# A language-model tower: values product with swapped operands on 32-column tiles, second bias in the accumulation, second norm on ScalarE

## The chip, the cores and the metric

The program runs on one core of one Trainium2 chip. The metric is the device time of one execution in microseconds; three timed executions of the kernel before gave 2760.56, 2769.51 and 2775.77 us, median 2769.51. The engines are named PE (TensorE, matrix products into PSUM), DVE (VectorE), ACT (ScalarE), POOL (GpSimd) and SP (SyncE, which starts DMAs).

## The reference

32 sequences of 512 tokens, each with 128 features, go through an embedding, three attention and feed-forward layers, and a routed expert layer:

```python
h = encoded(byte embedding, hashed 3- to 8-gram embeddings)      # 6 gathers of 128 floats per token
X = layernorm(h)
for l in range(3):
    Xn = layernorm(X) * ln1_w + ln1_b
    Q, K = rotary(Xn @ WQ), rotary(Xn @ WK); V = Xn @ WV         # 4 heads of 32 features
    A = (Q @ K.T) * decay mask                                   # causal, no softmax
    Y = A @ V                                                    # per head
    Yn = (Y - mean) / sqrt(var + eps), per head, * gn_w + gn_b
    G = Xn @ WG
    Y = (G * sigmoid(G) * Yn) @ WO + X
    X = gelu(layernorm2(Y) @ w1 + b1) @ w2 + b2 + Y
h = h + X
out = h + expert[argmax(layernorm(h) @ Wg + bg)](layernorm(h))   # 8 experts, 128 -> 256 -> 128
```

All of it is fp32. Means are taken out of the weights ahead of time (the output projection, w2, b2 and V's weights are centred), so a norm in the layers needs only a mean of squares.

## The kernel before

**Tiling.** A sequence is four chunks of 128 tokens, and two sequences are in flight: stream s = 0, 1 takes the sequences 2*it + s for it = 0..15 ("pairs"). Each stream is worked in two halves h of two chunks each. So there are four interleaved work lines (s, h), and 16 x 3 x 4 = 192 passes of one half through one layer. Each half has two PSUM banks, a and b. The state of earlier chunks (K transposed times V, 128x128, masked to the heads) carries attention from chunk to chunk; within a chunk the scores are computed and masked.

**One layer of one half** is `attend` and then `feed`, written once per engine:
- DVE normalises X (L860), PE transposes it, ACT copies it with weight and bias to `xT` (L674).
- PE: Q and K, V, and the gate (L1154 to L1158). DVE: rotary products (L920 to L924) and the swish `sw` (L928). ACT: V and the tanh (L682, L683).
- PE transposes Q and K (L1165); ACT copies them out, Q four times with one head's rows kept (L686, L688). PE computes the state (V and K), then the scores (128x512 per chunk); DVE masks both (L934 to L945).
- PE, values (from L1178): per chunk, the product with the state, and then for each head the masked scores `A` (128x128, the stationary operand) with V's 32 columns moving, accumulated in bank a. Tokens lie on partitions.
- ACT squares y (L693), DVE sums the squares per head (L950), POOL adds eps and takes the power -1/2 (L606, L607), DVE multiplies y with it into `xn` (L954), PE transposes it, ACT applies gn_w and gn_b into `zp` (L697), DVE multiplies with `sw` (L960), PE multiplies with WO, DVE adds X into `Y1` (L963).
- `feed`: ACT square sums of Y1 (L667), POOL power (L579), DVE norm (L860), PE transposes, ACT copy; PE w1 into both banks, ACT gelu (L712), PE w2 into bank a; POOL adds the second bias to Y1 into `Y1b` (L616); DVE adds bank a and Y1b into X (L975).

**Order.** Every engine runs its stages in a fixed order, found when the program is built: `by_progress` (L380) always takes the stage with the smallest point next. A stage is what stands between two `yield`s; the yielded number is its point within `attend` or `feed`, to which the start of the part and the lag of the half (`START`, `HLAG`, L59 and L60) are added; `attend` is 29.8 and `feed` 14.4 long (L369). Beside the layers run `embed` (gathered rows summed, transposed, encoded, normed) and `route` (router norm, logits, places, scatter), and on POOL the gathers (L561), 12 per half and pair. Engines meet only at semaphores (`wait_ge`, `then_inc`); an engine that waits holds all that is behind it in its order.

**Around the layers.** Until the first gathered rows arrive the engines hash the n-grams and prepare weights (DVE L754 to L857). After the last pair, 40 tiles of 512 rows go through the experts in loops.

All PE matmuls of this text have L1097 in the profile (the helper `mm`), the transposes L1116 or L1165, so they are told apart by their tiles, written out<-moving,stationary.

## Time and profile before

| | |
|---|---|
| median of the timed runs | 2769.51 us |
| the profiled execution: its own time | 2767.15 us |
| span, first to last instruction | 2765.3 us |
| granted TensorE clock, mean | 0.972 |
| PE busy | 2505.9 us (91%) |
| PEld (weight loads) busy | 2123.8 us (77%) |
| DVE busy | 2042.8 us (74%) |
| POOL busy | 1984.1 us (72%) |
| ACT busy | 1557.8 us (56%) |

The span is what one profiled execution took between its first and last instruction. Busy is the time covered by an engine's instructions; a matmul's record runs from its start to its modelled end, so records of successive matmuls overlap. PEld runs beside PE. A line in a group of instructions gives their number behind an x and the mean duration of one in ns.

### The profile page before, as it was taken

The page shows a single profiled execution, that of the slowest core. Times are in us where ns is not written, and L with a number is a line of the kernel's source. Part 1 is how long each engine was busy: PE and PEld are TensorE (multiplying, and loading weights), DVE is VectorE, ACT ScalarE, POOL GpSimd, SP SyncE. Part 2 cuts the span into 40 slices and gives each one's busy share as a digit, 9 for nine tenths or more (in the row PEclk, how much of TensorE's full clock was granted, in tenths as well). Part 3 has the DMA queues.
Part 4 walks back from the last instruction along what each step waited for, and adds up shares of the span by engine and source line. Part 5 has one row for each costly group of instructions (what it writes and reads, how often), then busy time and mean ns, then how long its engine had stood idle before and what let it go on. Part 6 is the DMA issues. An engine that isn't in the chain of part 4 may idle for free.

```text
span 2765.3 us, 49055 instructions
## 1 busy us (share of the span) xinstructions
PE 2505.9 (91%) x16336; PEld 2123.8 (77%) x16336; DVE 2042.8 (74%) x6261; ACT 1557.8 (56%) x4733; POOL 1984.1 (72%) x2286
## 2 busy tenths in 40 slices
PE   0499999999999999999999999999999999977775
PEld 0378888888888888888888888888888888865553
DVE  5368888888787878787878887887888797764443
ACT  0156666666666666666666666666666666542332
POOL 4787777777777787868787777777787854445666
PEclk9799999999999999999999999999999999988897
DMA  4521110202021202111111112020211000003443
GB/s 158 203 72 58 61 63 27 95 25 98 26 95 29 95 27 73 49 61 63 60 62 61 62 41 81 25 98 27 95 29 33 27 17 22 7 8 108 141 133 105
DMA packets 107320, 181.25 MB, mean 66 GB/s; under 512 B 23748, under 2 KB 46406, under 8 KB 106960
## 3 DMA queue, kind: packets, MB, share of 16 engines
q1 hardware_dynamic: 73296, 110.87, 11.8%
q0 software_dynamic: 33792, 67.45, 8.3%
q8 instruction: 125, 2.05, 0.3%
q14 instruction: 107, 0.88, 0.1%
HBM read 89.54 MB, written 90.78 MB: 65 GB/s over the span
## 4 chain that ended last, share of the span: by engine, by line
PE 68%; POOL 14%; DVE 7%; issue 6%; another core or an unknown queue 2%; DMA 1%; ACT 1%; SPq 1%; POOLq 0%; ACTq 0%; DVEq 0%
PE psum L1097 61%; POOL grams L568 6%; PE psum L1116 4%; POOL gr L607 3%; PE psum L1165 3%; POOL side_rstd L586 1%; POOL routed_rows L627 1%; POOL rstd L579 1%; DVE hid L945 1%; DMA grams<-expert_w 1%; DVE side_n L874 1%; ACT sq L693 1%; PE psum L1111 1%; DVE xn L860 0%
## 5 line engine op out<-in xcount | busy, mean ns | idle before, releaser
L568 POOL DMA_INDIRECT grams<-gram_table,idx_all x768 | 780.0, 1016 | 195.5 <-issue 184.5
L1097 PE MATMUL psum<-xT,lw 128*128 128x256 f32 x1920 | 487.9, 385 | 11.9 <-ACT xT L674 8.5
L1097 PE MATMUL psum<-lw,hid 128*128 128x129 f32 x3072 | 409.6, 276 | 1.7 <-ACT hid L712 1.7
L579 POOL TENSOR_TENSOR rstd<-ss,con 128x2 f32<-128x2 f32 x320 | 230.3, 720 | 251.4 <-ACT squares L667 230.8
L1097 PE MATMUL psum<-qm,qkT 128*128 128x512 f32 x768 | 371.8, 607 | 23.6 <-DVE kv L934 21.0
L1097 PEld LDWEIGHTS psum<-lw,hid 128*128 128x128 f32 x3072 | 381.6, 192 | 9.0 <-ACT hid L712 3.8
L1097 PE MATMUL psum<-V,hid 128*128 128x32 f32 x3072 | 383.0, 269 | 5.7 <-issue 3.2
L1097 PEld LDWEIGHTS psum<-V,hid 128*128 128x128 f32 x3072 | 375.1, 192 | 12.8 <-issue 12.1
L1097 PEld LDWEIGHTS psum<-xT,lw 128*128 128x128 f32 x1920 | 339.7, 193 | 50.2 <-ACT xT L674 13.0
L712 ACT ACTIVATE hid<-psum,par 128x256 f32<-128x256 f32 x768 | 317.9, 474 | 49.8 <-PE psum L1097 44.3
L607 POOL TENSOR_TENSOR gr<-ms,con 128x8 f32<-128x8 f32 x192 | 324.6, 1691 | 16.0
L688 ACT ACTIVATE qm<-psum,con 128x256 f32<-128x256 f32 x768 | 303.5, 497 | 0.0
L1097 PE MATMUL psum<-lw,xT 128*128 128x256 f32 (+1 forms) x1536 | 293.5, 335 | 0.7 <-ACT xT L674 0.7
L674 ACT ACTIVATE xT<-psum,par 128x256 f32<-128x256 f32 x384 | 213.0, 564 | 132.7 <-PE psum L1116 129.5
L945 DVE TENSOR_TENSOR hid<-psum,con 128x512 f32<-128x512 f32 x384 | 258.4, 687 | 27.8 <-PE psum L1097 20.3
L1097 PEld LDWEIGHTS psum<-lw,xT 128*128 128x128 f32 x1536 | 257.8, 196 | 25.8 <-ACT xT L674 1.1
L1116 PE MATMUL psum<-con,xn 128*128 128x128 f32 x1152 | 223.9, 281 | 21.8 <-DVE xn L860 14.9
L693 ACT ACTIVATE sq<-psum 128x256 f32<-128x256 f32 x192 | 73.8, 384 | 279.3 <-PE psum L1097 254.6
L1097 PEld LDWEIGHTS psum<-qm,qkT 128*128 128x128 f32 x768 | 131.8, 192 | 122.4 <-issue 119.4
L1116 PEld LDWEIGHTS psum<-con,xn 128*128 128x128 f32 x1152 | 154.3, 153 | 76.3 <-DVE xn L860 32.3
L897 DVE SCALAR_TENSOR_TENSOR side_n<-grams,gate,side_n 128x128 f32<-128x128 f32 x640 | 193.3, 359 | 0.0
L667 ACT ACTIVATE squares<-Y 128x129 f32<-128x129 f32 x384 | 117.6, 315 | 119.0 <-DVE Y L963 101.0
(176 smaller groups left out, 4832.7 us busy)
## 6 DMA issues: line engine op xcount, KB each, us to landing
routed_rows<-pad SPq DMA_DIRECT2D x265, 264.0 KB
grams<-expert_w SPq DMA_DIRECT2D x44, 321.0 KB
grams<-gram_table,idx_all POOLq DMA_INDIRECT x768
grams<-routed_rows SPq DMA_DIRECT2D x44, 264.0 KB
xb<-x SPq DMA_DIRECT2D x32, 256.0 KB
lw<-layer_w SPq DMA_DIRECT2D x1, 2503.5 KB, 12.0
routed_rows<-row,slot POOLq DMA_INDIRECT x128
con<-consts SPq DMA_DIRECT2D x1, 1339.5 KB, 6.0
```

The lines of the kernel that those rows point to most:

```text
L568: pool.indirect_dma_start(grams[s][:, g, c, :], None, gram_table, bass.IndirectOffsetOnAxis(ap=idx_all[:, g, at:at + 1], axis=0))\
L579: pool.tensor_tensor(rstd[s][:, CS[h]], ss[s][:, CS[h]], const("half")[:, 0:2], ALU.pow)\
L607: pool.tensor_tensor(gr[s][:, c], ms[s][:, c], const("half")[:, 0:n], ALU.pow).then_inc(y_r[s], 1)
L667: last = act.activation(scratch[s][:, c, :], src[s][:, c, 1:], ACT.Square, scale=float(H) ** -0.5, accum_out=dst[s][:, c:c + 1])
L674: act.activation(xT[s][:, TS[h]], src[:, 0:2 * P], ACT.Identity, bias=b, scale=w).then_inc(xT_s[s][h], 1)
L688: last = act.activation(qm[s][:, h, n, :], bank_b(s, h)[:, 0:2 * P], ACT.Copy, scale=const("heads")[:, n * HD:n * HD + 1])
L693: act.activation(sq[s][:, CS[h], :], chunks(bank_a(s, h))[:, 0:2, :], ACT.Square, scale=float(HD) ** -0.5).then_inc(y_sq[s], 1)
L712: last = act.activation(hid[s][:, h, 2 * m + f, :], src[:, f * 2 * P:(f + 1) * 2 * P], ACT.Gelu, bias=param("ffn_b1", l * FB + 2 * m + f))
L897: last = dve.scalar_tensor_tensor(acc[:, c, :], grams[s][:, g, c, :], w, acc[:, c, :], ALU.mult, ALU.add)
L945: dve.tensor_tensor(A[s][:, h, m], chunks((a, b)[m]), causal.unsqueeze(1).to_broadcast([P, HEADS, P]), ALU.mult).then_inc(sc_s[s], 1)
L1097: return pe.matmul(dst, lhsT, rhs, start=start, stop=stop)
L1116: last = pe.transpose(dst[:, (c % 2) * P:(c % 2 + 1) * P], src[:, c, :], eye)
```

## The change

- **Values product.** The operands are swapped: V's 32 columns of a head are stationary, the head's 128x128 masked scores move, and the result is written to that head's 32 partitions of bank a. y now lies transposed (features on partitions, tokens along the row). The state product is swapped likewise and moved ahead of both chunks.
- **Norm of y.** The sum of squares per head is a matmul of `sq` with four columns of the head mask; DVE adds eps; POOL takes the power; ACT spreads the result over each head's 32 columns into `xn`; PE transposes that; ACT multiplies it with gn_w; DVE multiplies it with y (bank a) and then adds gn_b and multiplies with `sw`.
- **Second bias.** In setup DVE splits the centred bias into three bf16 parts, one per partition 0 to 2 of `bias2`. After the w2 matmuls, two bf16 matmuls with a stationary matrix whose first three rows are ones add it in the accumulation. POOL's add is gone and DVE adds Y1 itself.
- **Second norm** (`feed`): applied by ACT in two instructions of 128 columns instead of by DVE in one of 256.
- **Stage points.** One number per layer instead of one for all in `attend` and `feed`; other points in `embed`, `route` and the later gathers; lags written out per half. The lengths of the parts are unchanged.

```diff
-START = (0, 28.01)
-HLAG = 12.18
+LATER_GATHERS = (8.16, 13.29, 18.32, 29.07, 53.32, 54.86, 60.54, 79.31, 82.83, 96.37, 105.71, 109.59)
+LAGS = ((0, 12.38), (28.17, 40.59))
...
# gpsimd: gathered
-                    yield (1.25 * n - 15, 4.2 * n, 9.5 * n)[min(it, 2)]
+                    yield (1.25 * n - 15, 4.2 * n, LATER_GATHERS[n])[min(it, 2)]
# gpsimd: attend
-                yield -2.74
+                yield (2.93, -3.28, -3.65)[l]
...
                 pool.wait_ge(y_ms[s], nth(k, 2, h))
-                link(pool.tensor_scalar(ms[s][:, c], ms[s][:, c], EPS, 1.0, ALU.add, ALU.mult))
                 pool.tensor_tensor(gr[s][:, c], ms[s][:, c], const("half")[:, 0:n], ALU.pow).then_inc(y_r[s], 1)
# gpsimd: feed
-                yield 4.41
-                pool.wait_ge(y1_s[s], nth(k, 2, h))
-                pool.tensor_tensor(Y1b[s][:, CS[h], :], Y1[s][:, CS[h], 0:WIDE],
-                                   param("ffn_b2", l, WIDE).unsqueeze(1).to_broadcast([P, 2, WIDE]), ALU.add)\
-                    .then_inc(y1b_s[s], 1)
# scalar: new helper, and attend
+            def norm_apply(s, h, src, scale):
+                for c in half_chunks(h):
+                    last = act.activation(xn[s][:, c, :], src[s][:, c, 1:WIDE], ACT.Copy, scale=scale[s][:, c:c + 1])
+                last.then_inc(n_out[s][h], 1)
...
-                yield 21.47
-                act.wait_ge(yT_p[s], nth(k, 2, h))
-                act.activation(zp[s][:, TS[h]], bank_b(s, h)[:, 0:2 * P], ACT.Identity,
-                               bias=param("gn_b", l), scale=param("gn_w", l)).then_inc(z_a[s], 1)
+                yield (24.89, 24.28, 23.58)[l]
+                act.wait_ge(y_r[s], nth(k, 2, h))
+                act.activation(xn[s][:, CS[h], :].rearrange("p c (n d) -> p (c n) d", d=HD),
+                               gr[s][:, h * n:(h + 1) * n].unsqueeze(2).to_broadcast([P, n, HD]), ACT.Copy)\
+                   .then_inc(y_rb[s], 1)
+                yield (27.81, 27.37, 25.91)[l]
+                act.wait_ge(rT_y[s], nth(k, 2, h))
+                act.activation(zp[s][:, TS[h]], bank_b(s, h)[:, 0:2 * P], ACT.Copy,
+                               scale=param("gn_w", l)).then_inc(z_a[s], 1)
# scalar: feed
-                yield 1.18
+                yield (-71.44, 3.64, 4.99)[l]
+                act.wait_ge(n_rstd[s][h], nth(it, OWN, 2 * l))
+                norm_apply(s, h, Y1, rstd)
+                yield (5.94, 5.85, 8.36)[l]
                 norm_T(it, s, 2 * l + 1, h, bank_b(s, h), param("ln2_w", l), param("ln2_b", l))
# vector: setup
+                rest = param("ffn_b2")
+                for n in range(3):
+                    link(dve.tensor_copy(bias2_part[n][:, :], rest))
+                    if n < 2:
+                        link(dve.tensor_tensor(bias2_rest[:, :], rest, bias2_part[n][:, :], ALU.subtract))
+                        rest = bias2_rest[:, :]
+                link(dve.tensor_scalar(bias2[:, :], bias2_part[0][:, :], eye[:, 0:1], None, ALU.mult))
+                for n in (1, 2):
+                    link(dve.scalar_tensor_tensor(bias2[:, :], bias2_part[n][:, :], eye[:, n:n + 1], bias2[:, :],
+                                                  ALU.mult, ALU.add))
+                link(dve.tensor_scalar(below_three[:, :], const("vocab"), 3.0, None, ALU.is_lt))
+                dve.tensor_scalar(three_bf[:, :], ones_bf[:, :], below_three[:, :], None, ALU.mult)
# vector: attend
-                dve.wait_ge(y_sq[s], nth(k, 2, h))
-                dve.tensor_reduce(ms[s][:, h * n:(h + 1) * n], sq[s][:, cs, :].rearrange("p c (n d) -> p (c n) d", d=HD),
-                                  axis=AX_X, op=ALU.add).then_inc(y_ms[s], 1)
-                yield 18.66
-                dve.wait_ge(y_r[s], nth(k, 2, h))
-                dve.tensor_tensor(xn[s][:, cs, :].rearrange("p c (n d) -> p (c n) d", d=HD),
-                                  a[:, 0:2 * P].rearrange("p (n d) -> p n d", d=HD),
-                                  gr[s][:, h * n:(h + 1) * n].unsqueeze(2).to_broadcast([P, n, HD]), ALU.mult)\
-                   .then_inc(y_n[s], 1)
+                dve.wait_ge(ms_p[s], nth(k, 2, h))
+                dve.tensor_scalar(ms[s][:, h * n:(h + 1) * n], a[:, 2 * P:2 * P + n], EPS, None, ALU.add)\
+                   .then_inc(y_ms[s], 1)
...
-                dve.tensor_tensor(zp[s][:, ts], zp[s][:, ts], sw[s][:, ts], ALU.mult).then_inc(z_s[s], 1)
+                link(dve.tensor_tensor(zp[s][:, ts], a[:, 0:2 * P], zp[s][:, ts], ALU.mult))
+                dve.scalar_tensor_tensor(zp[s][:, ts], zp[s][:, ts], param("gn_b", l), sw[s][:, ts], ALU.add, ALU.mult)\
+                   .then_inc(z_s[s], 1)
# vector: feed
-                dve.wait_ge(n_rstd[s][h], nth(it, OWN, 2 * l))
-                norm_apply(s, h, Y1, rstd)
...
-                dve.tensor_tensor(X[s][:, cs, 0:WIDE], wide(bank_a(s, h)), Y1b[s][:, cs, :], ALU.add).then_inc(x_s[s], 1)
+                dve.tensor_tensor(X[s][:, cs, 0:WIDE], wide(bank_a(s, h)), Y1[s][:, cs, 0:WIDE], ALU.add).then_inc(x_s[s], 1)
# tensor: attend
                 pe.wait_ge(kv_s[s], nth(k, 2, h))
+                pe.wait_ge(sc_s[s], nth(k, 4, 2 * h))
+                for c in half_chunks(h):
+                    if c:
+                        mm(a[:, chunk(c % 2)], kv[s][:, c - 1, :], qkT[s][:, h, 0, c % 2, :], c < 3, False)
                 for c in half_chunks(h):
                     i = c % 2
                     pe.wait_ge(sc_s[s], nth(k, 4, c))
-                    if c:
-                        mm(a[:, chunk(i)], qkT[s][:, h, 0, i, :], kv[s][:, c - 1, :], True, False)
                     for n in range(HEADS):
-                        last = mm(a[:, i * P + n * HD:i * P + (n + 1) * HD], A[s][:, h, i, n, :],
-                                  V[s][:, c, n * HD:(n + 1) * HD], c == 0, c == 0 or n == HEADS - 1)
+                        d = slice(n * HD, (n + 1) * HD)
+                        last = mm(a[d, chunk(i)], V[s][:, c, d], A[s][:, h, i, n, :], False, i == 1)
                 last.then_inc(y_p[s], 1)
-                yield 20.53
-                pe.wait_ge(y_n[s], nth(k, 2, h))
+                yield (22.81, 20.21, 20.43)[l]
+                pe.wait_ge(y_sq[s], nth(k, 2, h))
+                for c in half_chunks(h):
+                    last = mm(a[:, 2 * P + c % 2 * HEADS:2 * P + (c % 2 + 1) * HEADS], sq[s][:, c, :],
+                              const("heads").rearrange("p (n d) -> p n d", d=HD)[:, :, 0])
+                last.then_inc(ms_p[s], 1)
+                yield (26.25, 26.56, 25.13)[l]
+                pe.wait_ge(y_rb[s], nth(k, 2, h))
...
-                half_transposes(b, xn[s], h).then_inc(yT_p[s], 1)
+                half_transposes(b, xn[s], h).then_inc(rT_y[s], 1)
# tensor: feed
+                for i in range(2):
+                    last = mm(wide(a)[:, i, :], three_bf[:, :], bias2[:, l * WIDE:(l + 1) * WIDE], False, i == 1)
                 last.then_inc(ff_p[s], 1)
```

## Rows read from the trace of the kernel before

**Rows 1.** Busy time of each engine by stretch (x instructions), granted clock, DMA share
```profile
core 0: us, PE busy (x) PEld busy (x) DVE busy (x) ACT busy (x) POOL busy (x), PEclk, DMA share, GB/s
0.00:82.00 82.00, 5.55 (x20) 3.79 (x20) 43.83 (x143) 2.96 (x8) 41.01 (x46) 1.00 0.52 193
200.00:2240.00 2040.00, 1991.59 (x13359) 1712.37 (x13357) 1643.94 (x5014) 1284.15 (x4011) 1568.47 (x1836) 1.00 0.17 56
2465.00:2765.00 300.00, 203.27 (x1045) 148.58 (x1044) 127.07 (x443) 82.25 (x138) 178.08 (x174) 0.85 0.39 114
```
**Rows 2.** The page: the chain that ended last, by engine
```profile
PE 68%; POOL 14%; DVE 7%; issue 6%; another core or an unknown queue 2%; DMA 1%; ACT 1%; SPq 1%; POOLq 0%; ACTq 0%; DVEq 0%
```
**Rows 3.** The page: the values product's group (busy, mean ns, idle before)
```profile
L1097 PE MATMUL psum<-V,hid 128*128 128x32 f32 x3072 | 383.0, 269 | 5.7 <-issue 3.2
```
**Rows 4.** PE in order of time, 1241 to 1244 us: start, length, group
```profile
1241.93 0.17 PE L1097 MATMUL psum<-pick_bf,before_bf 128*128 128x16 bf16 x1
1241.96 0.17 PE L1097 MATMUL psum<-pick_bf,ones_bf 128*128 128x16 bf16 x1
1241.98 0.47 PE L1097 MATMUL psum<-kv,qkT 128*128 128x128 f32 x2
1242.29 0.98 PE L1097 MATMUL psum<-V,hid 128*128 128x32 f32 x8
1243.10 0.47 PE L1097 MATMUL psum<-kv,qkT 128*128 128x128 f32 x2
1243.40 0.98 PE L1097 MATMUL psum<-V,hid 128*128 128x32 f32 x8
1244.22 1.96 PE L1097 MATMUL psum<-qm,qkT 128*128 128x512 f32 x4
```
**Rows 5.** PE in order of time, 1224 us
```profile
1224.06 0.51 PE L1097 MATMUL psum<-par,side_T 128*128 128x8 f32 x4
1224.43 0.81 PE L1097 MATMUL psum<-lw,hid 128*128 128x129 f32 x5
```
**Rows 6.** PE in order of time, 37 to 39 us
```profile
37.04 1.51 PE L1103 MATMUL psum<-con,hid 128*128 128x128 f32 x6 [37.04 <-DVE hid L814]
38.48 0.69 PE L1097 MATMUL psum<-par 128*64 128x128 f32 x2
```
**Rows 7.** Waits, 200 to 2240 us: who for whom, total us, times, longest
```profile
PEld psum L1116 <- DVE xn L860: 21.6, 37, 1.5
PEld psum L1097 <- DVE zp L960: 9.8, 36, 1.3
PEld psum L1097 <- ACT xT L674: 9.1, 13, 0.7
```
**Rows 8.** DVE groups, 200 to 2240 us
```profile
L960 DVE TENSOR_TENSOR zp<-zp,sw 128x256 f32<-128x256 f32 x167 | 70.7, 423 | 9.9 <-ACT zp L697 9.9
L954 DVE TENSOR_TENSOR xn<-psum,gr 128x256 f32<-128x256 f32 x167 | 69.7, 418 | 79.2 <-POOL gr L607 77.8
L950 DVE TENSOR_REDUCE ms<-sq 128x8 f32<-128x256 f32 x167 | 69.6, 417 | 82.5 <-ACT sq L693 80.2 <-issue 0.2
L860 DVE TENSOR_TENSOR xn<-Y,rstd 128x256 f32<-128x256 f32 x167 | 69.2, 414 | 0.8 <-POOL rstd L579 0.8
```
**Rows 9.** ACT groups, 200 to 2240 us
```profile
L667 ACT ACTIVATE squares<-Y 128x129 f32<-128x129 f32 x336 | 102.7, 314 | 103.4 <-DVE Y L963 85.9 <-issue 13.8
L682 ACT ACTIVATE V<-psum 128x256 f32<-128x256 f32 x167 | 64.2, 384 | 159.2 <-PE psum L1097 155.1 <-issue 4.1
```
**Rows 10.** POOL groups, 200 to 2240 us
```profile
L579 POOL TENSOR_TENSOR rstd<-ss,con 128x2 f32<-128x2 f32 x280 | 201.2, 719 | 170.1 <-ACT squares L667 149.9 <-DMA routed_rows<-pad 15.0 <-issue 3.0
L616 POOL TENSOR_TENSOR Y1b<-Y,par 128x258 f32<-128x258 f32 x166 | 117.4, 707 | 2.0
L606 POOL TENSOR_SCALAR ms<-ms 128x8 f32<-128x8 f32 x167 | 33.8, 202 | 69.2 <-DVE ms L950 59.2
```
**Rows 11.** DVE in order of time, 42 to 61 us
```profile
42.10 0.56 DVE L838 TENSOR_TENSOR par<-par 128x384 f32<-128x384 f32 x1
60.67 0.48 DVE L893 TENSOR_SCALAR side_n<-grams,gate 128x128 f32<-128x128 f32 x2 [6.62 <-DMA grams<-gram_table,idx_all]
```

More of the change, by code:

```diff
@@ L194, in tower_program @@
         Y1 = two(sb, "Y1", [P, CH, WIDE + 1])
-        Y1b = two(sb, "Y1b", [P, CH, WIDE])
+        bias2 = sb("bias2", [P, LAYERS * WIDE], BF16)
+        bias2_part = [sb(f"bias2_part{n}", [P, LAYERS * WIDE], BF16) for n in range(3)]
+        bias2_rest = sb("bias2_rest", [P, LAYERS * WIDE])
+        three_bf = sb("three_bf", [P, P], BF16)
+        below_three = sb("below_three", [P, 1])
         xn = two(sb, "xn", [P, CH, H])
@@ L304, in tower_program @@
         xT_s = halves("norm_transpose_ready")
-        qk_p = two(sem, "qk_in_psum")
-        g_p = two(sem, "v_and_g_in_psum")
+        proj_p = two(sem, "qk_then_v_and_g_in_psum")
         tg_s = two(sem, "v_and_gate_tanh_ready")
@@ L318, in tower_program @@
         y_sq = two(sem, "y_squared")
-        y_ms = two(sem, "y_square_sums")
+        y_ms = two(sem, "y_square_sums_ready")
         y_r = two(sem, "y_rstd_ready")
-        y_n = two(sem, "y_normed")
-        yT_p = two(sem, "y_transposed")
-        z_a = two(sem, "y_affine_ready")
+        ms_p = two(sem, "y_square_sums_in_psum")
+        rT_y = two(sem, "y_rstd_transposed")
+        y_rb = two(sem, "y_rstd_spread")
+        z_a = two(sem, "y_scale_ready")
         z_s = two(sem, "z_ready")
@@ L326, in tower_program @@
         y1_s = two(sem, "attention_residual_ready")
-        y1b_s = two(sem, "bias2_added")
         f_p = two(sem, "ffn_hidden_in_psum")
@@ L409, in main_program @@
         def main_program(embed, attend, feed, route, *others):
-            streams = [(s, h, START[s] + h * HLAG) for s in range(2) for h in range(2)]
+            streams = [(s, h, LAGS[s][h]) for s in range(2) for h in range(2)]
             by_progress(*[one_by_one(lag + FIRST, *sequences(s, h, attend, feed)) for s, h, lag in streams],
@@ L589, in embed @@
             def embed(it, s, h):
-                yield 44.48
+                yield 46.56
                 side_norm_rstd(it, s, 0, h)
-                yield 52.47
+                yield 55.56
                 pool.wait_ge(x0_ss[s], nth(it, 2, h))
@@ L714, in feed @@
                     last.then_inc(f_s[s], 1)
-                yield 9.97
+                yield (14.14, 13.47, 13.63)[l]
                 if l < LAYERS - 1:
@@ L720, in route @@
             def route(it, s, h):
-                yield 19.16
+                yield 23.33
                 act.wait_ge(rT_p[s], nth(it, 2, h))
@@ L878, in embed @@
             def embed(it, s, h):
-                yield 0.39
+                yield 18.2
                 dve.wait_ge(x_in[s], (it + 1) * 16)
@@ L909, in attend @@
                 a, b = bank_a(s, h), bank_b(s, h)
-                yield -2.66
+                yield (1.17, 2.95, 3.97)[l]
                 if l == 0:
@@ L916, in attend @@
                     norm_apply(s, h, X, rstd)
-                yield 4.81
-                dve.wait_ge(qk_p[s], nth(k, 2, h))
+                yield (8.82, 9.44, 9.84)[l]
+                dve.wait_ge(proj_p[s], nth(k, 4, 2 * h))
                 dve.tensor_tensor(qk[s][:, cs, :], b.rearrange("p (c n) -> p c n", c=2), cos_v[:, cs, :], ALU.mult)
@@ L929, in attend @@
                    .then_inc(sw_s[s], 1)
-                yield 8.95
+                yield (15, 14.24, 15.7)[l]
                 own = (2, 1)[h]
@@ L1011, in route @@
                    .then_inc(r_pk[s], 1)
-                yield 57.38
+                yield 68.43
                 dve.wait_ge(r_pos[s], nth(it, 2, h))
@@ L1126, in embed @@
             def embed(it, s, h):
-                yield 22.35
+                yield 25.96
                 pe.wait_ge(acc_step[s][h], (it + 1) * (2 * NG))
@@ L1144, in attend @@
                 a, b = bank_a(s, h), bank_b(s, h)
-                yield 0.13
+                yield (2.41, 4.21, 4.29)[l]
                 norm_T(it, s, 2 * l, h, a)
-                yield 3.05
+                yield (5.12, 6.88, 7.41)[l]
                 pe.wait_ge(xT_s[s][h], nth(it, NORMS, 2 * l))
@@ L1155, in attend @@
                     last = mm(b[:, (c % 2) * 2 * H:(c % 2 + 1) * 2 * H], xT[s][:, chunk(c)], lw[:, l, LW["qk"]])
-                last.then_inc(qk_p[s], 1)
+                last.then_inc(proj_p[s], 1)
                 for c in half_chunks(h):
                     mm(a[:, chunk(c % 2)], xT[s][:, chunk(c)], lw[:, l, LW["v"]])
-                mm(a[:, 2 * P:], lw[:, l, LW["g"]], xT[s][:, TS[h]]).then_inc(g_p[s], 1)
-                yield 7.08
+                mm(a[:, 2 * P:], lw[:, l, LW["g"]], xT[s][:, TS[h]]).then_inc(proj_p[s], 1)
+                yield (12.22, 11.19, 11.52)[l]
                 pe.wait_ge(rope[s], nth(k, 2, h))
@@ L1166, in attend @@
                 last.then_inc(qkT_p[s], 1)
-                yield 8.1
+                yield (13.18, 13.36, 13.34)[l]
                 pe.wait_ge(sw_s[s], nth(k, 2, h))
@@ L1220, in feed @@
                     if f % 2 == 0:
-                        yield (6.36, 7.86)[f // 2]
+                        yield ((12.06, 9.7, 12.44), (12.49, 12.19, 12.69))[f // 2][l]
                         pe.wait_ge(f_s[s], nth(k, 4, 2 * h + f // 2))
                     for i in range(2):
-                        last = mm(wide(a)[:, i, :], hid[s][:, h, f, chunk(i)], w2[:, f, :], f == 0 and i == 0,
-                                  f == FB - 1 and i == 1)
+                        mm(wide(a)[:, i, :], hid[s][:, h, f, chunk(i)], w2[:, f, :], f == 0 and i == 0, False)
+                for i in range(2):
+                    last = mm(wide(a)[:, i, :], three_bf[:, :], bias2[:, l * WIDE:(l + 1) * WIDE], False, i == 1)
                 last.then_inc(ff_p[s], 1)
@@ L1229, in route @@
                 k, b = (it + 1) * LAYERS, bank_b(s, h)
-                yield 16.1
+                yield 22.49
                 pe.wait_ge(r_n[s], nth(it, 2, h))
@@ L1241, in route @@
                 last.then_inc(r_lg[s], 1)
-                yield 56.86
+                yield 65.87
                 pe.wait_ge(r_pk[s], nth(it, 2, h))
```

72 lines of the change are left out of this document (37 added, 35 removed).

## The prediction

> **What bounds the kernel now.** I read the stretches first [rows 1]. Until 82 us TensorE is nearly idle (5.6 us busy): hashing and the first gathers. After 2465 us come the expert tiles. Neither holds a changed instruction, apart from the setup discussed below. Between 200 and 2240 us TensorE is busy 1991.6 of 2040 us, at a granted clock of 1.00, which is the 2.4 GHz level. VectorE is busy for 1643.9 us, GpSimd for 1568.5, ScalarE for 1284.2. The chain of waits gives 68% of the span to PE, 14% to POOL and 7% to DVE [rows 2]. So TensorE sets the pace of the layers, and the others matter where they make it wait.
>
> The unit of work is one half (two 128-token chunks) of one stream through one layer; I call it a block. ScalarE writes V once per block, 167 times in this stretch [rows 9], so a block takes 2040/167 = 12.2 us. The whole program has 192 blocks (the page counts 3072 records of the values product, 16 per block [rows 3]). Each 0.1 us of TensorE time per block is thus 19 us of the total. The profiled execution took 2767.2 us (span 2765.3), 2.4 us below the median 2769.5 of the timed runs; I sum against 2767.
>
> **TensorE, part by part.** An fp32 matmul is two records (8 values matmuls per block are 1536, and the page counts 3072 records). Their pace must be read from start to start, since the busy times overlap (a record "lasts" 269 ns and the next starts long before).
>
> *Values product.* Now each head's masked scores are the 128x128 stationary operand and 32 columns of V move. In the timeline [rows 4] 4 records of the state product and 16 of the values product fill 1241.98 to 1244.22 us: 2.24 us for 20 records, 0.112 us each. A record with 32 moving columns costs as much as one with 128, so loading the stationary tile is what it costs. 16 x 0.112 = 1.79 us per block. Afterwards V's 32 columns stand still and the 128 columns of the scores move, 16 records again. Three outcomes:
> - Nothing overlaps: each record streams 128 columns, at 0.112 us [rows 4]: 1.79 us, no gain.
> - The four heads write four different groups of 32 output partitions, so a head can run beside another. The two records of one head use the same columns of the array and must follow each other. With instructions started in order, head n+1's first record can run beside head n's second, and no more. Each of 8 heads then adds one record, plus one at the end: 9 x 0.11 = 0.99 us.
> - All four heads run side by side: 16 x 0.112/4 = 0.45, with the tail 0.50 us.
>
> No row shows two matmuls side by side, so the ends are 0.50 and 1.79. I take 0.99, which asks only for disjoint output partitions and keeps the order: -0.80 us per block.
>
> *State product.* Operands swapped, 128 moving columns before and after, same number: 0. Its two matmuls now stand ahead of both chunks, which changes no wait but the place of one.
>
> *Mean squares.* The reduction leaves DVE and becomes two matmuls with 128 stationary and 4 moving columns, 4 records. The router's 128x8 matmuls are the same form [rows 5]: four take 0.37 us to the next start; at the loading pace of rows 4 they take 4 x 0.112 = 0.45. I take 0.45: +0.45.
>
> *Second bias.* Two bf16 matmuls, one record each, 129 moving columns. The bf16 records with 16 columns follow each other at 0.02 to 0.03 us [rows 4]; a fp32 record of 128 columns costs 0.112. I take half of the latter for each (one bf16 record, half of a split fp32 one): +0.11, with bounds 0.05 and 0.22.
>
> *Transposes.* As many as before (now of the spread reciprocal root instead of the normed y): 0.
>
> *Going in and out of narrow column tiles.* The trace has one place where the stationary width changes: from six 128-wide transposes to a 64-wide matmul at 38.48 us [rows 6]. The six records take (1.51-0.42)/5 = 0.22 us each, so the last begins at about 38.13, and the next starts 0.35 us later instead of 0.22: 0.13 us lost, at the 1.2 GHz level (the pace is twice that of rows 4). Two changes per block at between 0 and 0.27 us (a whole record's length [rows 3]) each; I take 0.08: +0.16.
>
> The Trainium skill speaks against the change here: "TensorEngine Tiling (Array Packing)", section Key Properties, says that changing the tiling mode drains the engine. The row above fits it in direction. A full drain of 0.27 us twice would make this term 0.54 instead of 0.16, and the sum +0.30 per block.
>
> Sum on TensorE: -0.80+0.45+0.11+0.16 = -0.08 us per block, 192 x -0.08 = -15 us.
>
> **The other engines.** DVE loses the reduction (0.417), the norm of y (0.418), the norm before the feed-forward (0.414) and the product with the swish (0.423); it gains an 8-column add from PSUM (between 0 and 0.42; I take 0.16) and two 256-column products (0.42 each, by the same rows) [rows 8]. Net -0.67 us per block: 9.8 becomes 9.2 of 12.2. ACT gains two 128-column scalings (0.31 each by the squares) and a 256-column spread (0.38 by the copy of V) [rows 9]: +1.0, 7.7 becomes 8.7. Bounds for it are 0.4 and 1.5, and at either end ACT stays under TensorE. POOL loses the bias add (0.707) and an add of eps (0.202) [rows 10]: 9.4 becomes 8.5. None of this counts directly.
>
> It counts where TensorE waits. The three largest waits that name another engine (xn from DVE 21.6, zp from DVE 9.8, xT from ACT 9.1 us) make 40.5 us in the stretch, 0.24 us per block [rows 7]. Two of them hang on DVE, the engine that gets lighter. The bias add on POOL also disappears between two queued gathers. I take half: -0.12 us per block, -23 us; bounds: -0.24, and a loss that is the fourth case below. The stage points only reorder the queues (gathers on POOL and side work too); their number is unchanged, and I give them no value of their own.
>
> What becomes late next: after y, the chain goes ACT square, PE, DVE add, POOL power, ACT spread, PE transposes, ACT scale, two DVE products, PE. That is one stop at the TensorE queue more, and one at ACT in place of one at DVE. In layer 0 the norm before the feed-forward is put right behind the square sums on ACT; ACT then stands still for POOL's power (0.719 us [rows 10]), and the other three streams' ACT work is queued behind it.
>
> **Setup.** Splitting the bias adds ten DVE instructions, eight of them 387 columns wide. A 384-column one takes 0.56 us [rows 11]: at most 5 us. DVE then idles 6.62 us for the first gathered rows, which hides it. Without that cover it would be +5 us.
>
> **Forecast.** -15 - 23 = -38 us: 2729 us.
>
> **Rivals.**
> - *All four heads side by side.* 0.50 instead of 0.99 us: another -0.49 x 192 = -94 us, 2635. For it: the output partitions of all four are disjoint. Against: it needs the two records of a head not to block the next one. The Trainium skill, "TensorE: Matmul & The Clock Gate", Part 3, has 2.38 times for three column tiles, which would bring 1.79 to about 0.75 us; no run here shows that yet.
> - *No overlap.* The moving operand costs what the loading did: 1.79 instead of 0.99, +154 us, 2883. For it: nothing in the trace overlaps two matmuls, and rows 4 show 128 moving columns at the same 0.112 us. Against: the stationary tile is four times narrower, so the loading is out of the way.
> - *The longer chain shows (the slower side).* Overlap as forecast, but the new stop and ACT's standing still make TensorE wait once more in two of three blocks, at the mean of the present xn wait (21.6/37 = 0.58 us [rows 7]): 128 x 0.58 = +74, and the relief of 23 is gone: 2729+97 = 2826. It decides against the change from about +0.2 us of extra wait per block. For it: TensorE, saturated, is the engine where a further stop costs most, and the order is fixed. Against: four streams are in flight, so one has 4 x 12.2 = 49 us for a layer, and three engines have slack.
> - *It doesn't do what it says:* if the swapped matmuls run as full-width ones with only 32 columns used, that is the no-overlap case without the switches: 2883-31 = 2852. I count it there.
>
> **How the numbers follow.** Forecast 45%, all four 12%, no overlap 17%, longer chain 26%. The forecast's own range is 2670 to 2800: switches at 0 bring -31 us and at 0.54 us +73, relief at 0.24 us -23 and at 0 +23, the bias bounds -12 and +21, and they will not all fall on one side. The 80% range reaches into both neighbours: 2640 to 2875. About 0.5% is what a measurement of this kernel can tell from no change. Faster: 33 of the 45, the 12, and 5 of the last (a mild chain): 50%. Same: 9 of the 45 and 8 of the chain: 17%. Slower: the rest, 33%.
>
> **What would show it.** Right: 16 values records in about 1.0 us, starts of neighbouring heads nearly together and a head's two records 0.11 us apart; four 4-column records in 0.45 us; a gap of under 0.15 us on each side of the values group; block time about 12.0 us. Wrong: values at 0.11 us per record (no overlap), at 0.03 (all four), gaps of 0.25 us at the switches, or TensorE's idle time beyond the present 48 us with ACT or POOL named as releaser (longer chain).

## The result, and the profile after

The changed kernel takes 2639.85 us (median of four runs) against 2769.46 for the kernel before beside it: ratio 0.953, 95% interval 0.950 to 0.957, 130 us less. The forecast was 2729 (range 2640 to 2875); the rival with all four heads side by side said 2635. The profiled execution took 2644.05 us.

The page of the changed kernel, busy time by engine, answers to the table of the profile before. All engines but ACT are lighter:

```profile
PE 2393.8 (91%) x17488; PEld 1954.2 (74%) x17488; DVE 1903.8 (72%) x6079; ACT 1709.5 (65%) x5309; POOL 1818.0 (69%) x1902
```

By stretch (columns as in [rows 1]): the head of the program and the experts are about as long as before; the layers end at about 2340 us instead of 2465.

```profile
core 0: us, PE busy (x) PEld busy (x) DVE busy (x) ACT busy (x) POOL busy (x), PEclk, DMA share, GB/s
0.00:82.00 82.00, 6.25 (x22) 4.07 (x22) 48.47 (x153) 3.48 (x10) 42.97 (x49) 1.00 0.48 174
200.00:2140.00 1940.00, 1901.94 (x14379) 1575.06 (x14378) 1521.36 (x4864) 1418.51 (x4514) 1425.04 (x1500) 1.00 0.20 60
2340.00:2642.00 302.00, 205.46 (x1056) 147.66 (x1056) 126.87 (x445) 84.92 (x145) 177.94 (x175) 0.85 0.40 113
```

ACT's copy of V, once per block, gives the block time: 1940/168 = 11.55 us instead of 12.22, and 0.67 x 192 = 128 us.

```profile
L683 ACT ACTIVATE V<-psum 128x256 f32<-128x256 f32 x168 | 64.1, 382 | 91.2 <-PE psum L1117 89.3 <-issue 2.0
```

TensorE in order of time, changed kernel (start, length, group), the place that answers to [rows 4]:

```profile
1201.46 0.61 PE L1117 MATMUL psum<-lw,zp 128*128 128x129 f32 x4
1201.91 0.61 PE L1117 MATMUL psum<-qkT,kv 128*128 128x128 f32 x4
1202.44 0.65 PE L1117 MATMUL psum<-hid,V 128*32 128x128 f32 x16
1203.02 0.44 PE L1136 MATMUL psum<-con,xn 128*128 128x128 f32 x2
1203.29 0.39 PE L1117 MATMUL psum<-par,side_T 128*128 128x128 f32 x2
...
1204.40 0.51 PE L1117 MATMUL psum<-con,sq 128*128 128x4 f32 x4
...
1212.90 0.28 PE L1117 MATMUL psum<-bias,three_bf 128*128 128x129 bf16 x2
1213.02 1.95 PE L1117 MATMUL psum<-xT,lw 128*128 128x256 f32 x8
```

All 16 values records fit into 0.65 us, of which the last one's own length is 0.27: their starts span 0.38 us, four waves of four at one record's pace (0.11). The waves can be counted: cut into windows of 0.11 to 0.12 us, four more values records have started in each (a window's count holds all records that run in it, here also the earlier ones):

```profile
core 0: us, PE busy (x), PEclk, DMA share, GB/s
1202.38:1202.50 0.12, 0.06 (x4) 1.00 0.00 0
1202.50:1202.62 0.12, 0.12 (x8) 1.00 0.00 0
1202.62:1202.73 0.11, 0.11 (x12) 1.00 0.00 0
1202.73:1202.84 0.11, 0.11 (x16) 1.00 0.00 0
```

The state and values products together take 1203.02 - 1201.91 = 1.11 us; in [rows 4] they took 2.24. The place is typical: over the whole stretch, from each record's start to the next one's, the two products took 2.11 us per block before and take 1.02 now (half of the blocks have one state product, the other half two).

The row also shows both changes of tile width. The fourth state record starts at about 1202.24 (three paces of 0.112 after 1201.91) and the first values record 0.20 later, 0.09 more than the pace. The last values record starts at about 1202.82 and the next group 0.20 later: 0.09 again. The two records behind it take 0.27 instead of 0.22, another 0.05. Together 0.24 us per block in and out. The 0.05 need not belong to the change of width: in [rows 4] the state product's two records behind values records took 0.30 as well (1243.10 to 1243.40), in full-width tiles. Without it the two changes cost 0.18.

### The profile page after: what moved, and what is told of

It reads as the page before. It is cut to its first block, busy times and chain, and to the rows that moved or that the text cites. A ratio compares the mean times of both kernels' runs of the same rounds, so it can differ in the third digit from the quotient of the medians.

```text
span 2642.1 us, 51369 instructions
## 1 busy us (share of the span) xinstructions
PE 2393.8 (91%) x17488; PEld 1954.2 (74%) x17488; DVE 1903.8 (72%) x6079; ACT 1709.5 (65%) x5309; POOL 1818.0 (69%) x1902
## 4 chain that ended last, share of the span: by engine, by line
PE 72%; POOL 8%; DVE 6%; ACT 4%; issue 4%; another core or an unknown queue 3%; DMA 1%; SPq 1%; ACTq 0%; DVEq 0%; POOLq 0%
PE psum L1117 62%; PE psum L1136 6%; POOL grams L571 3%; PE psum L1185 3%; POOL gr L609 2%; POOL rstd L582 1%; DVE side_n L924 1%; ACT qm L689 1%; DMA grams<-expert_w 1%; ACT squares L663 1%; PE psum L1131 1%; ACT xT L675 1%; ACT xn L669 1%; DVE hid L972 1%
## 5 line engine op out<-in xcount | busy, mean ns | idle before, releaser
L571 POOL DMA_INDIRECT grams<-gram_table,idx_all x768 | 793.2, 1033 | 200.1 <-issue 189.8
L1117 PE MATMUL psum<-lw,hid 128*128 128x129 f32 x3072 | 392.6, 276 | 8.7 <-ACT hid L722 8.7
L1117 PEld LDWEIGHTS psum<-lw,hid 128*128 128x128 f32 x3072 | 368.1, 192 | 14.0 <-ACT hid L722 11.3
L609 POOL TENSOR_TENSOR gr<-ms,con 128x8 f32<-128x8 f32 x192 | 320.1, 1667 | 77.5 <-DVE ms L977 75.2
L1117 PEld LDWEIGHTS psum<-lw,xT 128*128 128x128 f32 x1536 | 252.1, 192 | 52.3 <-issue 17.6
L669 ACT ACTIVATE xn<-Y,rstd 128x128 f32<-128x128 f32 x384 | 132.9, 394 | 131.1 <-POOL rstd L582 130.3
L1136 PEld LDWEIGHTS psum<-con,xn 128*128 128x128 f32 x1152 | 134.3, 146 | 83.2 <-DVE xn L887 24.3
L924 DVE SCALAR_TENSOR_TENSOR side_n<-grams,gate,side_n 128x128 f32<-128x128 f32 x640 | 176.7, 346 | 0.0
L995 DVE TENSOR_TENSOR X<-psum,Y 128x258 f32<-128x258 f32 x192 | 81.6, 425 | 113.2 <-PE psum L1117 111.2
L623 POOL DMA_INDIRECT routed_rows<-row,slot x128 | 130.2, 1018 | 42.3 <-issue 32.9
L683 ACT ACTIVATE V<-psum 128x256 f32<-128x256 f32 x192 | 73.3, 382 | 130.0 <-PE psum L1117 114.1
```

The costliest lines, as they stand in the source:

```text
L571: pool.indirect_dma_start(grams[s][:, g, c, :], None, gram_table, bass.IndirectOffsetOnAxis(ap=idx_all[:, g, at:at + 1], axis=0))\
L609: pool.tensor_tensor(gr[s][:, c], ms[s][:, c], const("half")[:, 0:n], ALU.pow).then_inc(y_r[s], 1)
L623: pool.indirect_dma_start(slots, bass.IndirectOffsetOnAxis(ap=slot[s][:, c:c + 1], axis=0), row[s][:, c, :], None).then_inc(r_done[s], 16)
L669: last = act.activation(xn[s][:, c, :], src[s][:, c, 1:WIDE], ACT.Copy, scale=scale[s][:, c:c + 1])
L924: last = dve.scalar_tensor_tensor(acc[:, c, :], grams[s][:, g, c, :], w, acc[:, c, :], ALU.mult, ALU.add)
L1117: return pe.matmul(dst, lhsT, rhs, start=start, stop=stop)
```

## The experiments

18 runs in five comparisons follow, each beside the kernel before on the same chip; the changed kernel is among them twice more, and two other kernels ran twice. Absolute times differ between chips (before: 2713 to 2789 us), so ratios to before are compared. The first comparison's chip is 2% faster, and ratios came out up to 0.8% lower on it: two kernels that ran on both kinds had 0.945 and 0.958 there, 0.954 and 0.961 elsewhere. The changed kernel itself ran three times at 0.953, 0.952 and 0.952.

### How many heads run side by side

One column group (in the changed kernel):

```
-  last = mm(a[d, chunk(i)], V[s][:, c, d], A[s][:, h, i, n, :], False, i == 1)
+  last = mm(a[0:HD, chunk(i)], V[s][:, c, d], A[s][:, h, i, n, :], n == 0, n == HEADS - 1)
```

> The changed kernel, with the results of all four heads written to output partitions 0 to 31, so that all heads use the same 32 columns of the array (three heads' results are lost). Theory (the gain is four heads side by side on TensorE): each of the 16 records now has to follow the one before, at 0.11 us: 1.79 instead of 0.44 us per block, +1.35 x 192 = +259 us, near 2899 us, above the kernel before. Rival (the gain came from the lighter DVE and POOL, and TensorE has room): TensorE absorbs most of it, under +100 us.

Measured: 2775.38 us, ratio 1.023 (1.021 to 1.025). Slower than the kernel before.

Two column groups: the output is `a[n // 2 * HD:(n // 2 + 1) * HD, ...]`, with the first head of each group starting the sum and the second ending it. In both kernels the state product is also closed by itself (flags True, True), since the values now overwrite part of it; the number and the size of the matmuls stay.

> The changed kernel with heads 0 and 1 on output partitions 0 to 31 and heads 2 and 3 on 32 to 63 (two heads' results are lost), so that two column groups are in use instead of four. Theory (one matmul per column group at a time, no order among groups): 8 waves of two records, 0.88 us per block instead of 0.44; +0.44 x 192 = +84 us on TensorE, of which the run with one group suggests about three quarters reach the total: +60 us, ratio to before 0.975. Rival (in order, only the neighbour overlaps): 0.99 us or more per block, and the same with four groups.

Measured: 2686.52 us, ratio 0.969 (0.966 to 0.972), 1.7% or 46 us on the changed kernel.

TensorE in order of time, first with one group, then with two; the last column's counts are the same 16 records:

```profile
1213.09 0.39 PE L1117 MATMUL psum<-qkT,kv 128*128 128x128 f32 x2
1213.41 1.94 PE L1117 MATMUL psum<-hid,V 128*32 128x128 f32 x16
1215.27 0.44 PE L1136 MATMUL psum<-con,xn 128*128 128x128 f32 x2
```

```profile
1206.68 0.47 PE L1117 MATMUL psum<-qkT,kv 128*128 128x128 f32 x2
1207.08 1.09 PE L1117 MATMUL psum<-hid,V 128*32 128x128 f32 x16
1208.10 0.44 PE L1136 MATMUL psum<-con,xn 128*128 128x128 f32 x2
```

To the next group's start that is 1.86 us with one column group, 1.02 with two, 0.58 with four (changed kernel, 1202.44 to 1203.02): the time goes with the number of records per group. The theory of free column groups had +0.44 and +1.35 us per block; +0.44 and +1.28 came. Swapping the operands without the overlap would have lost: the 16 values records of the kernel before took 0.81 us twice in [rows 4], 1.62, and one group takes 1.86.

How much of that reaches the total is another matter. TensorE's busy time in the same 1940 us, for the changed kernel (above), with two visits (below), two groups and one group:

```profile
200.00:2140.00 1940.00, 1920.51 (x14171) 1549.70 (x14170) 1497.49 (x4787) 1399.76 (x4452) 1400.43 (x1483) 1.00 0.19 60
```

```profile
200.00:2140.00 1940.00, 1931.37 (x14125) 1620.70 (x14124) 1495.86 (x4773) 1397.61 (x4438) 1402.17 (x1480) 1.00 0.19 60
```

```profile
200.00:2140.00 1940.00, 1939.99 (x13344) 1660.21 (x13343) 1412.60 (x4504) 1323.97 (x4190) 1330.34 (x1392) 1.00 0.18 57
```

The changed kernel leaves TensorE idle for 38 us of them, 0.2 us per block. Added work fills this first: of two groups' 84 us, 46 came, and of the other 38 us the idle time that is gone makes 34 (0.23 us per block against 0.05). With one group there is no idle time left, and of 246 us (1.28 x 192) about 215 came, against 0.944 of before for the changed kernel on that chip (an estimate from the head-by-head kernel's two ratios). There the idle time explains only part of the rest: on that chip the head-by-head kernel, as fast as the changed one, leaves TensorE idle for 11 of 1900 us.

### Whether the order of the matmuls matters

```
-  for c in half_chunks(h):
-      i = c % 2
-      pe.wait_ge(sc_s[s], nth(k, 4, c))
-      for n in range(HEADS):
+  pe.wait_ge(sc_s[s], nth(k, 4, 2 * h + 1))
+  for n in range(HEADS):
+      for c in half_chunks(h):
+          i = c % 2
           ...
```

> The changed kernel with the values matmuls ordered head by head (chunk 0, chunk 1 of head 0, then head 1, ...) instead of four heads of one chunk at a time; both chunks' masks are waited for first. Theory A (matmuls start in the order of the program, each waiting for its own columns): four records in a row use the same columns, a new head starts beside the last of them: 13 x 0.11 = 1.43 us per block instead of 0.44, +190 us, 2830. Theory B (the order in the program does not matter, the four column groups run on their own): 0.44 us again, within 0.5% of 2640 plus what the earlier wait costs (under 10 us).

> The head-by-head order once more, now beside the changed kernel on one chip. If order is nothing to the four column groups: within 0.5% of the changed kernel (the 0.945 of the first experiment was then the other chip). If adjacent matmuls on the same columns help: 20 us below it.

Measured: 0.945 on the first chip, then 0.954 (0.952 to 0.955) beside the changed kernel's 0.952 (0.950 to 0.954): the same. In the trace (second run) the group is as short as in the changed kernel, though in the program four records in a row belong to the same columns:

```profile
1208.07 0.61 PE L1117 MATMUL psum<-qkT,kv 128*128 128x128 f32 x4
1208.61 0.67 PE L1117 MATMUL psum<-hid,V 128*32 128x128 f32 x16
1209.20 0.44 PE L1136 MATMUL psum<-con,xn 128*128 128x128 f32 x2
```

Counted in windows of the same width, here too four more records have started in each:

```profile
1208.55:1208.67 0.12, 0.06 (x4) 1.00 0.00 0
1208.67:1208.79 0.12, 0.12 (x8) 1.00 0.00 0
1208.79:1208.90 0.11, 0.11 (x12) 1.00 0.00 0
1208.90:1209.01 0.11, 0.11 (x16) 1.00 0.00 0
```

Started in the order of the text it would have taken 1.43 us, since with one column group a record started only every 0.11 us. So the records do not start in the order in which the kernel's text has the matmuls. Whether they are reordered when the program is compiled or in the engine, the trace doesn't tell.

The earlier wait alone, in the original order, and the base of that comparison:

> The changed kernel itself, as the base for the other runs of this comparison (the chips differ by up to 2% in absolute time). Ratio to the kernel before 0.953, as in the first comparison; 0.945 would mean that ordering the values product head by head (ratio 0.945 in the first experiment) brought nothing beyond a difference between chips.

> The changed kernel, waiting for both chunks' masked scores before the first values matmul, in the original order of the matmuls. If the earlier wait is what made the head-by-head order 0.8% faster than the changed kernel, this one is as fast as that (0.945 of before). If the order did it, this one is like the changed kernel. The theory that order does not matter to the four column groups expects the first, or no difference between all three.

Measured: 0.952 (0.949 to 0.956) for the changed kernel and 0.953 (0.950 to 0.957) with the earlier wait: no difference. The base of the next comparison:

> The changed kernel, base of this comparison: 0.953 of the kernel before.

Measured: 0.952 (0.950 to 0.954), 2653.89 us.

### The price of going in and out

```
-  for c in half_chunks(h):
-      if c:
-          mm(a[:, chunk(c % 2)], kv[s][:, c - 1, :], qkT[s][:, h, 0, c % 2, :], c < 3, False)
   for c in half_chunks(h):
       i = c % 2
       pe.wait_ge(sc_s[s], nth(k, 4, c))
+      if c:
+          mm(a[:, chunk(i)], kv[s][:, c - 1, :], qkT[s][:, h, 0, i, :], True, False)
       ...
```

> The changed kernel with each chunk's state product right before that chunk's values again, so TensorE goes in and out of narrow column tiles twice per block. Theory (a change in and out costs 0.10 + 0.15 us, as the trace of the changed kernel shows around the values group): +0.25 x 192 = +48 us, 2688. Rival (a full drain of 0.27 us each way): +104 us, 2744. Second rival (free): within 0.5%.

> Two visits to the narrow tiles per block once more, beside the changed kernel on one chip. Theory (0.10 us in, 0.15 us out): +48 us on the changed kernel. Rival (full drain of 0.27 us each way): +104. Rival (free, hidden in TensorE's waits): within 13 us.

Measured: 0.958 on the first chip; then 0.961 (0.960 to 0.963), 2682.93 us, 29 us above the changed kernel. TensorE in order of time (second run):

```profile
1204.23 0.39 PE L1117 MATMUL psum<-qkT,kv 128*128 128x128 f32 x2
1204.55 0.43 PE L1117 MATMUL psum<-hid,V 128*32 128x128 f32 x8
1204.90 0.49 PE L1117 MATMUL psum<-qkT,kv 128*128 128x128 f32 x2
1205.32 0.43 PE L1117 MATMUL psum<-hid,V 128*32 128x128 f32 x8
1205.67 1.98 PE L1117 MATMUL psum<-qm,qkT 128*128 128x512 f32 x4
```

1.44 us for what takes 1.11 in the changed kernel: 0.33 us per further visit, where the theory had 0.25, and 29 of 63 us reach the total. Of the other 34 us, 21 are idle time that is gone (0.23 us per block against 0.12); the rest isn't traced. On the first chip, with less idle time, the same edit cost 34 us (0.958 against 0.945). A drain of 0.27 us each way (+104 us in the total) is out: the row has 0.33 us for a visit where it would be 0.54.

### The second bias and the second norm

Undone in the changed kernel: both, then the bias alone, then the norm alone with its stage 0.8 to 1.6 later on DVE, then both with that later stage (and the bias 0.7 later in layer 2):

> The changed kernel with the second bias added on POOL again and the second norm applied on DVE again: what is left of the change is the swapped values product with its norm, and the points. Theory (TensorE alone sets the pace): it saves the two bias matmuls (0.13 us per block, -24 us) and pays little for the rest: 2615 to 2650. Rival (DVE and POOL had to be relieved): DVE +0.41 and POOL +0.71 us per block make TensorE wait: over 2680.

> The changed kernel with the second bias added by POOL again. TensorE loses two bf16 matmuls (0.13 us per block), POOL gains 0.71 us per block and the residual add waits for it. Theory (TensorE's work sets the pace): -24 us. Rival (POOL and the wait on it were what held the layers; it would explain most of the 190 us that both parts undone cost): +50 us or more.

> The changed kernel with the second norm on DVE again, its stage placed 0.8 to 1.6 later than in the run with both parts undone, so that DVE stands less behind POOL's power. Theory (the 190 us of that run came from DVE standing behind POOL's power in its fixed order, and with it everything queued on DVE): +60 to +190 us, with 'DVE xn waits for POOL rstd' above 100 us in the middle stretch. Rival (only the 0.41 us of DVE work per block counts): under +30 us.

> The changed kernel with both parts undone as in the first experiment, but with the norm's stage on DVE 0.8 to 1.6 later and the bias a little later in layer 2. Alone, the two undone parts cost 27 and 48 us. If these add and the first run's 7% came from the placing: +75 us on the changed kernel, ratio 0.98. If the two parts are what keeps DVE and POOL out of the way together: as slow as the first run, ratio 1.02.

Done alone in the kernel before, and both together:

> The kernel before with only the second bias moved into the accumulation (its own points otherwise). TensorE +0.13 us per block (+24 us), POOL -0.71 us per block and one wait less. By the theory that TensorE's work sets the pace: +10 to +24 us. By the theory that POOL's queue was holding TensorE up: -20 us or more.

> The kernel before with only the second norm moved from DVE to ACT at the same stage point. No TensorE work changes; DVE -0.41, ACT +0.79 us per block. Theory (a lighter DVE makes TensorE wait less): -10 to -40 us. Rival (ACT now stands behind POOL's power, with the other streams' work behind it): slower by 10 us or more.

> The kernel before with both the second bias in the accumulation and the second norm on ACT, with its own stage points. If the two gains (0.8% and 0.5% alone) add: 0.987 of before. If both relieve the same waits: 0.99.

| kernel | ratio to before | interval |
|---|---|---|
| changed, both undone | 1.025 (first chip) | 1.023 to 1.026 |
| changed, bias on POOL | 0.962 | 0.958 to 0.965 |
| changed, norm on DVE, later | 0.969 | 0.965 to 0.972 |
| changed, both undone, norm later | 0.998 | 0.997 to 0.999 |
| before, bias in the accumulation | 0.992 | 0.989 to 0.995 |
| before, norm on ACT | 0.995 | 0.993 to 0.996 |
| before, both | 0.993 | 0.991 to 0.995 |

In the kernel before, the two are worth 0.8% and 0.5%, and 0.7% together (19 us): they don't add. As the bias matmuls add about 0.12 us per block, 23 us, to TensorE there too, about 42 us of waiting went away, more than the 23 that the prediction gave the whole change. In the changed kernel, undoing the bias costs 27 us although TensorE loses work (the first expectation had -24, its rival 50 or more), undoing the norm 48 us, and both about 126 us (0.998 against 0.952), nearly the whole gain and midway between the two expectations. In the first placing it was about 218 us, by the same estimate of 0.944 for the changed kernel on the first chip. The waits of the 1940 us (who for whom, total, times, longest), first placing, where [rows 8] has 0.8 us for the second kind in the kernel before:

```profile
ACT V L690 <- PE psum L1124: 202.7, 134, 3.2
DVE xn L891 <- POOL rstd L584: 175.7, 122, 2.8
...
PE psum L1124 <- DVE hid L976: 98.9, 63, 2.2
```

and with the norm later:

```profile
DVE xn L891 <- POOL rstd L584: 109.9, 78, 2.8
```

There DVE stands still for POOL's power with the other streams' work behind it, and TensorE waits for that work (98.9 us for DVE's `hid` in the first placing, 37.4 in the later one, 1.3 in the changed kernel): it is busy for 1794 and 1810 us of the 1940, instead of 1902:

```profile
200.00:2140.00 1940.00, 1794.35 (x12959) 1470.98 (x12958) 1491.55 (x4635) 1216.87 (x3861) 1451.24 (x1540) 0.98 0.19 58
```

```profile
200.00:2140.00 1940.00, 1810.47 (x13304) 1475.63 (x13304) 1557.07 (x4768) 1243.12 (x3957) 1493.64 (x1576) 1.00 0.19 59
```

In the first placing the granted clock is 0.98 in this stretch, in the later one 1.00, so a part of the first one's cost can be the clock.

With the norm alone on DVE, the wait I had expected above 100 us is not among the largest of that stretch; the cost was still 48 us. TensorE is busy for 1877 of the 1940 us there, 25 less than in the changed kernel; which wait that goes back to is open. The parts can't be priced apart from the order they stand in. For the same reason the swapped product's own share of the 130 us is not measured: the runs with both other parts undone keep it, but under points made for a kernel with them.

### The stage points

> The changed kernel with one stage point per stage, the mean over the three layers, instead of one per layer (for ScalarE's second norm the mean of layers 1 and 2). Prediction's view (points only reorder, worth nothing of their own): within 15 us of the changed kernel. Rival (the points by layer hold a good part of the gain): +40 us or more.

> The changed kernel with layer 2's stage points in all three layers: a self-consistent set, unlike the means, which put stages of one chain out of step. If the order by layer matters of itself: over +40 us on the changed kernel. If only the means were a bad order: within +40 us.

Measured: 1.092 (1.088 to 1.096), 392 us above the changed kernel, and 1.130 (1.126 to 1.133). The same instructions, in another order, lose three to four times what the change won. The granted clock of the stretch is 0.97 in both, which can be part of the loss. With layer 2's points everywhere TensorE is busy for 1667 of 1940 us, and one wait is by far the largest:

```profile
200.00:2140.00 1940.00, 1667.25 (x11688) 1327.29 (x11687) 1244.01 (x3955) 1136.84 (x3675) 1145.19 (x1218) 0.97 0.17 53
```

```profile
POOL rstd L582 <- ACT squares L663: 489.5, 126, 8.5
...
ACT sq L694 <- PE psum L1117: 209.6, 116, 3.8
DVE sw L955 <- ACT tg L684: 190.4, 57, 5.6
```

In the changed kernel the first of these is 180.5 us. This doesn't show that points by layer are better than a good set without layers: neither of the two sets was fitted. It shows that a change of order can cost more than any edit here gains, and, with the 19 and the 126 us above, that an edit undone under an order made for it can seem worth more than it is alone.

## Why the prediction was wrong

The direction, the engine that sets the pace and the source of the gain (heads side by side) held; how many heads run side by side did not, and with it the size. Step by step, per block. "Over the stretch" means: from each TensorE record's start to the next one's, less the idle time, summed over the stretches of 2040 and 1940 us and divided by their 167 and 168 blocks.

- **Values product, the step that failed.** Forecast: "With instructions started in order, head n+1's first record can run beside head n's second, and no more", 0.99 us. The records of all four heads run side by side, 0.45 us by the pace (0.58 to the next group's start, the change of width included), and the order of the program's text doesn't matter. The state and values products with both switches went from 2.24 to 1.11 us in the rows and from 2.11 to 1.02 over the stretch: -1.09, where the forecast had -0.80 + 0.16 = -0.64. That is 86 us. I had put the rival at 12% because it needs the two records of a head not to block the next, and no row of the trace could show that.
  The Trainium skill, "TensorE: Matmul & The Clock Gate", Part 3, describes tiles of different columns running side by side but matmuls starting and ending strictly in order. The first half agrees with the 16 records in 0.65 us. The second half doesn't hold for the order of the kernel's text: by that, the head-by-head kernel would have been slower, and it was not. For the order of the compiled instructions no run here shows it either way.
- **Switches.** Forecast 0.16, read 0.18 to 0.24 for one visit, 0.33 for a further one. The place that the forecast took its 0.08 from, at 38 us, is no good measure: it took the slow pace there for the 1.2 GHz level, while the profile gives a granted clock of 1.00. The Trainium skill's drain ("TensorEngine Tiling (Array Packing)", Key Properties) is seen, as gaps of 0.20 us between starts where the pace is 0.11, but at less than half the 0.54 us that a whole record's length each way would be.
- **Mean squares.** Forecast 0.45, 0.40 over the stretch (the four records are 0.51 us long in the row above, the last one's own length included, as the router's in [rows 5]): 0.05 less.
- **Second bias.** Forecast 0.11, read 1213.02 - 1212.90 = 0.12 us, and 0.12 over the stretch: held. The other engines' work came out near the sums: ACT 1418.5/168 = 8.4 us per block (forecast 8.7), DVE 9.1 (9.2), POOL 8.5 (8.5).
- **Relief.** TensorE's terms over the stretch sum to -1.09 + 0.40 + 0.12 = -0.57, or -109 us. The block shortened by 0.67. Of the other 0.10, 0.06 is idle time (48 us of 2040 before, 38 of 1940 after), and 0.04 is records of the other groups that start sooner behind one another. The forecast had -0.12, near enough, but not for its reason: its 40.5 us were waits of the weight loads (PEld), and TensorE's own waits were smaller. They changed hands, from DVE to ACT, before:

```profile
PE psum L1116 <- DVE xn L860: 7.5, 15, 1.3
PE psum L1097 <- DVE hid L945: 6.1, 14, 0.4
```

  and after:

```profile
PE psum L1117 <- ACT hid L722: 7.7, 5, 1.8
PE psum L1117 <- ACT qm L689: 7.3, 15, 0.5
```

  All waits of this kind for DVE went from 17.6 to 3.0 us, those for ACT from 6.0 to 26.6.
- **Stage points, a term put at nothing without a reason.** "I give them no value of their own." An order can cost 15 to 19% here. What the new points gave against the old ones isn't known: no run has the changed kernel under the old points.
- **The longer chain** did not show with these points, though ACT stood still for POOL's power as the rival had it, for 112.7 us of the stretch. With both parts undone that chain of y is still there, and TensorE waits; whether for it or for the norm's return to DVE, those runs don't separate.
- **Setup** was hidden, as forecast: DVE's wait for the first gathered rows shrank from 6.62 to 1.35 us, and TensorE's first product of the layers starts at 82.09 us instead of 83.75.

The size was off by 89 us of 130. By the terms over the stretch, 86 came from the values product with its switches and 10 from the squares; the bias and the relief took 6 back. The measured time lies 0.15 us below the lower end of the range.

None of the kernels tried beats the changed one, measured beside it, beyond the intervals.

## What to carry to other kernels

Where a matmul with few moving columns pays for loading a wide stationary tile, ask whether swapping the operands gives disjoint groups of output partitions; in this kernel the gain came from the number of groups that run at once, not from the narrower load, and without the overlap the swap lost. On a saturated engine inside a fixed order, price a change in three parts: the work read from start to start, the idle time that swallows the first of it (here about half of the added 0.33 and 0.44 us per block), and the order itself, which here could cost more than either. Undo a part in both directions, in the old kernel and in the new one: 19 us in one and 126 in the other is the sign that it is the order, or the interplay, that is measured.

## What the runs showed of the hardware

- Column groups of 32 run fp32 matmuls side by side: 16 records of 128 moving columns take 1.86, 1.02 and 0.58 us to the next group's start with one, two and four groups.
- Their order in the kernel's text is without effect: 0.954 against 0.952 of before.
- A visit to narrow tiles costs 0.18 to 0.33 us, in and out: starts 0.20 us apart where the pace is 0.11.
- Two bf16 matmuls of 129 moving columns take 0.12 us, 0.06 each, where one fp32 matmul (two records) of 128 takes 0.22.
- Chips differ: the kernel before took 2713 us on one and 2768 to 2789 on others; the head-by-head kernel was granted a clock of 1.00 (2.4 GHz) in the layers on both kinds. Ratios moved by up to 0.8%.
